# A hybrid of convolution, masked attention and gated blocks on one core: attention scores by 32-row strips, transposed before the exponential, divided at the output

## The reference

```python
x = x + conv(group_norm(x), weight)          # 51x51 depthwise
t = to_tokens(x)                             # (16, 256, 32)
t = t + masked_attention(layer_norm(t))      # spikes of a scan pick the visible columns
t = t + ffn_steps(layer_norm(t))
# masked_attention, per image:
scores = Q @ K.T / sqrt(32), -inf where the mask or the spikes forbid it
w = nan_to_num(softmax(scores)); out = (w @ V) @ Wo + bo
# ffn_steps: 33 steps, each
op = argmax(h[0, 0, :19])                    # the first token of the first image picks the weights
if attn_mask[op]: h = softmax(q @ k.T * scale) @ v @ wo[op]
if ffn_mask[op]:  h = relu(h @ w1[op] + b1[op]) @ w2[op] + b2[op]
```

## Time and profile before

| what | us |
|---|---|
| three runs, median (lowest to highest) | 200.62 (198.45 to 200.82) |
| the profiled execution, span from its first to its last instruction | 199.1 |
| PE busy | 166.5 |
| DVE busy | 134.3 |
| ACT busy | 111.3 |
| POOL busy | 64.1 |

### The profile page before, as it was taken

The page is one execution under the profiler, slowest core; times in us unless marked ns, Lnnn a source line. Parts: engine busy times, 40 slices in busy tenths (PEclk is TensorE's granted clock), DMA queues, the critical chain, the costliest instruction groups (busy, mean ns, idle before and its releaser), DMA issues.

```text
span 199.1 us, 4262 instructions
## 1 busy us (share of the span) xinstructions
PE 166.5 (84%) x1255; PEld 112.6 (57%) x1256; DVE 134.3 (67%) x382; ACT 111.3 (56%) x324; POOL 64.1 (32%) x153
## 2 busy tenths in 40 slices
PE   7999989693898998879929679999867699998770
PEld 5779744241685776647412468776533587775320
DVE  1364578819938889896506388898756689789481
ACT  3464511429767656555405568675655877664670
POOL 8940000100061555453600005655510036556300
PEclk9999999969579999999966999999999999999997
DMA  5900000000000000000000100000000000000003
GB/s 158 315 3 0 3 0 3 0 3 2 0 2 0 2 0 3 0 0 18 3 7 2 20 0 0 0 0 0 0 0 15 0 0 0 0 0 0 0 0 110
DMA packets 3020, 3.33 MB, mean 17 GB/s; under 512 B 889, under 2 KB 2361, under 8 KB 3002
## 3 DMA queue, kind: packets, MB, share of 16 engines
q1 hardware_dynamic: 2858, 2.85, 4.8%
q10 hardware_dynamic: 144, 0.25, 0.4%
HBM read 2.58 MB, written 0.53 MB: 16 GB/s over the span
## 4 chain that ended last, share of the span: by engine, by line
PE 60%; DVE 16%; issue 9%; ACT 8%; POOL 2%; DVEq 1%; ACTq 1%; POOLq 0%
PE bank L555 17%; PE bank L528 8%; PE bank L615 5%; PE bank L542 5%; ACT qz L981 4%; PE bank L679 4%; PE bank L813 3%; PE bank L512 3%; DVE big L1269 3%; PE bank L633 3%; PE bank L600 2%; POOL prob L448 2%; PE bank L694 2%; ACT qz L1050 1%; ACT prob L905 1%
## 5 line engine op out<-in xcount | busy, mean ns | idle before, releaser
L448 POOL TENSOR_SCALAR prob<-prob,einv 128x256 f32<-128x256 f32 x96 | 44.7, 478 | 60.6 <-DVE einv L1264 60.4
L1269 DVE COPY big<-bank 128x512 f32<-128x512 f32 x48 | 32.9, 685 | 5.7 <-PE bank L528 5.7
L905 ACT ACTIVATE prob<-bank,nmax 128x256 f32<-128x256 f32 x64 | 29.8, 473 | 11.6 <-DVE nmax L1256 11.6
L528 PE MATMUL bank<-ident,prob 128*128 128x128 f32 x192 | 30.2, 280 | 6.5 <-POOL prob L448 6.4
L555 PE MATMUL bank<-hT,qz 128*128 128x256 f32 x128 | 32.7, 383 | 0.0
L528 PEld LDWEIGHTS bank<-ident,prob 128*128 128x128 f32 x192 | 21.4, 140 | 18.2 <-POOL prob L448 14.1
L1256 DVE TENSOR_REDUCE nmax<-bank 128x2 f32<-128x512 f32 x32 | 21.6, 687 | 4.8 <-PE bank L555 4.6
L555 PEld LDWEIGHTS bank<-hT,qz 128*128 128x128 f32 x128 | 22.3, 190 | 3.6 <-issue 1.6
L905 ACT ACTIVATE prob<-minus,nmax 128x256 f32<-128x256 f32 x32 | 16.0, 500 | 8.9 <-DVE nmax L1253 7.9
L555 PE MATMUL bank<-kt,qz 128*128 128x256 f32 x64 | 16.5, 386 | 0.9 <-ACT prob L905 0.9
L905 ACT ACTIVATION_READ_ACCUMULATOR prob<-bank,nmax 128x1 f32 x64 | 12.9, 202 | 0.0
(11 more groups left out here) (173 smaller groups left out, 256.8 us busy)
## 6 DMA issues: line engine op xcount, KB each, us to landing
xrev<-xrev_dram SPq DMA_DIRECT2D x1, 512.0 KB, 4.5
xin<-xtok_dram SPq DMA_DIRECT2D x1, 512.0 KB, 5.0
out_dram<-outT SPq DMA_DIRECT2D x2, 256.0 KB, 3.3
maskc<-maskc_dram SPq DMA_DIRECT2D x1, 256.0 KB, 4.8
kx<-kx_dram ACTq DMA_DIRECT2D x1, 248.0 KB, 3.1
wx<-wx_dram SPq DMA_DIRECT2D x1, 216.0 KB, 2.9
constf<-constf_dram SPq DMA_DIRECT2D x1, 186.0 KB, 4.6
wa<-wa_dram SPq DMA_DIRECT2D x3, 56.0 KB, 1.8
```

The source lines that it names most:

```text
L448: last = nc.gpsimd.tensor_scalar(prob[b % NPB][:, ih, :], prob[b % NPB][:, ih, :], einv[:, b, ih:ih + 1], 1.0, ALU.mult, ALU.mult)
L528: mm = pe.transpose(bank[2 + b % 2][:, jh * S + ih * P:jh * S + (ih + 1) * P], prob[b % NPB][:, ih, jh * P:(jh + 1) * P], ident)
L905: e = nc.scalar.activation(prob[b % NPB][:, ih, :], scores, ACT.Exp, bias=nmax[:, b, ih:ih + 1], scale=-1.0 if masked else 1.0, accum_out= ...
L1269: nc.vector.tensor_copy(flat(probT[b % NTB]), bank[2 + b % 2][:, :]).then_inc(s_PT, 1)
```

## The change

1. Queries are stored as projected (`qT`, one instruction per group), and scores contract over 32 rows: `score_pe` uses the strip of its image, two images at a time, into banks 0 to 3.
2. In the masked attention the masked scores go to one of six buffers `sh`; in the loop ACT copies the scores there, and DVE takes the maximum from the copy. POOL subtracts the maximum in place. PE turns the shifted scores into banks 4 and 5, and ACT makes the exponential of 128x512 from PSUM straight into `probT` (16 buffers).
3. Row sums come from PE: the weighing gets as many matmuls again with a column of ones, into the other half of the same bank. In the masked attention a matmul of a tiny constant starts that sum. DVE takes the reciprocal of 128x256 and multiplies while it drains.
4. The sums of the residual move to POOL for groups 0 and 1 (after images 12 and 15) and stay on DVE for 2 and 3.
5. The loop's body has the plain block first, then reads kind again and goes on to the attention in the same pass. The exponential's table is asked for once ahead of the loop.
6. In a block with attention the outputs of groups 0 and 1 stand before the second half of the hidden layer, and the weighing of group 3 before them.
7. The ring of tasks has two banks; `w1` comes with `wf` already in four strips, placed by one copy, on POOL in blocks with attention. The memset of `qz` is gone.

```diff
-        RING = 3
-        SCORES = (0, 1, 4)
-        AHEAD = len(SCORES)
+        RING = 2
+        YBANKS = (6, 7)
...
-        ATTY = "AAAA"
+        ATTY = "DDDD"
-        LPRE = "ADAD" + "ADAD"
+        LPRE = "AAAA" + "ADAD"
...
-                    last = nc.gpsimd.tensor_scalar(prob[b % NPB][:, ih, :], prob[b % NPB][:, ih, :], einv[:, b, ih:ih + 1], 1.0,
-                                                   ALU.mult, ALU.mult)
+                    last = nc.gpsimd.tensor_scalar(sh[b % NSH][:, ih, :], sh[b % NSH][:, ih, :], nmax[:, b, ih:ih + 1], 1.0,
+                                                   ALU.subtract if masked else ALU.add, ALU.mult)
...
+        def score_pe(pe, b, h, keys):
+            g, rows, at_row = strip(b)
+            mm = pe.matmul(bank[b % 4][:, h * S:(h + 1) * S], qT[rows, g, h * P:(h + 1) * P], keys[rows, g, :],
+                           start=True, stop=True, tile_position=at_row)
+            if h == NH - 1:
+                mm.then_inc(s_S, 1)
+        def scores_pe(pe, bs, keys):
+            for h in range(NH):
+                for b in bs:
+                    score_pe(pe, b, h, keys)
...
         def weigh_pe(pe, base, t, k0, g):
+            t.drained(pe, k0 + max(g - 1, 0))
+            wait(pe, s_P, base, GB * (g + 1))
+            out = bank[YBANKS[g % 2]]
...
+            if t is st:
+                pe.matmul(out[:, S:2 * S], onesq[:, :], tiny[:, :], start=True, stop=False)
+            for jh in range(NH):
+                for q in range(GB):
+                    mm = pe.matmul(out[q * C:(q + 1) * C, S:2 * S], onesc[:, :], probT[g * GB + q][:, jh, :],
+                                   start=t is not st and jh == 0, stop=(jh == NH - 1), tile_position=(0, q * C))
...
+        def attention_pe(pe, base, t, k0, keys, ahead, masked):
+            ahead()
+            for n in range(B // 2):
+                if n + 2 < B // 2:
+                    wait(pe, s_nm if masked else s_cp, base, 2 * n + 2 - (0 if masked else B))
+                    scores_pe(pe, (2 * n + 4, 2 * n + 5), keys)
+                turn_pe(pe, base, 2 * n)
+                if n % 2 == 0 and n:
+                    weigh_pe(pe, base, t, k0, n // 2 - 1)
+                turn_pe(pe, base, 2 * n + 1)
...
+            def before_spikes():
+                scores_pe(pe, (0, 1, 2, 3), kt)
+                pe.wait_ge(s_spk, 1)
...
+                    def ahead():
+                        product_pe(pe, t, 0, bda[:, :], hT[:, 0, :], S)
+                        product_pe(pe, t, 1, bda[:, :], hT[:, 1, :], S)
+                        t.drained(pe, 1)
+                        scores_pe(pe, (0, 1, 2, 3), hT)
+                        product_pe(pe, t, 2, bda[:, :], hT[:, 2, :], S)
+                        product_pe(pe, t, 3, bda[:, :], hT[:, 3, :], S)
                         for g in range(NG):
                             values(t, NG + g, hT, g, bdv[:, :])
...
+                with pe.If(kind == 3):
...
+                    token0(r)
+                    hidden(r, 0)
+                    token0_row()
+                    weigh_pe(pe, att, t, len(LPRE), NG - 1)
+                    k = K_HF + GB + 1
+                    t.drained(pe, k - 1)
+                    outputs(t, k, (0, 1))
+                    t.drained(pe, k)
+                    hidden(r, 1)
...
+            def copy_scores(b):
+                wait(act, s_S, base, b + 1)
+                if b >= NSH:
+                    wait(act, s_T, base, b - NSH + 1)
+                nc.scalar.activation(flat(sh[b % NSH]), bank[b % 4][:, :], ACT.Copy).then_inc(s_cp, 1)
...
+                if not masked and b + 4 < B:
+                    copy_scores(b + 4)
+                wait(act, s_T, base, b + 1)
+                nc.scalar.activation(flat(probT[b]), bank[4 + b % 2][:, :], ACT.Exp, scale=-1.0 if masked else 1.0).then_inc(s_P, 1)
...
+            def normed_output(t, k, g, to):
+                t.filled(dve, k)
+                link(nc.vector.reciprocal(sinv[:, g, :], bank[YBANKS[g % 2]][:, S:2 * S]))
+                return nc.vector.tensor_tensor(to[:, g, :], bank[YBANKS[g % 2]][:, 0:S], sinv[:, g, :], ALU.mult)
...
+            def attention_dve(base, masked, output, early=()):
+                for b in range(B):
                     row_max(base, b, masked)
+                    if b == 3:
+                        for e in early:
+                            e()
+                    if b in (10, 14):
+                        output((b - 10) // GB)
```

More of the change, by code:

```diff
@@ L470, in _, with residual, residuals @@
                     nc.gpsimd.tensor_tensor(vg, vg, rep(bvo[:, :], GB), ALU.add).then_inc(s_vb, 1)
-            attention_pool(pool)
+            def residual(g):
+                wait(pool, s_dd, 0, count("D", STATIC[:K_ATT + g + 1]))
+                wait(pool, s_da, 0, count("A", STATIC[:K_ATT]))
+                nc.gpsimd.tensor_tensor(outT[:, g, :], outT[:, g, :], yn[:, g, :], ALU.add).then_inc(s_resP, 1)
+            def residuals(b):
+                if b >= 12 and (b - 12) % 3 == 0:
+                    residual((b - 12) // 3)
+            attention_pool(pool, True, residuals)
             reg_att = pool.alloc_register("pool_att")
@@ L716, in _, with first_token0 @@
             pe.wait_ge(s_tabmove, 32)
-            attention_pe(pe, 0, st, K_ATT, kt, spare)
+            def before_spikes():
+                scores_pe(pe, (0, 1, 2, 3), kt)
+                pe.wait_ge(s_spk, 1)
+                st.fill_wait(pe, K_CNT)
+                pe.matmul(st.bank(K_CNT)[:, 0:S], onesb[:, :], spk[:, :], start=True, stop=True).then_inc(s_task, 1)
+                for h in range(NH):
+                    transposed_pe(pe, K_RES + h, tok, h)
+                spare(bank[5], 6)
+            def first_token0():
+                pe.wait_ge(s_resP, 1)
+                pe.wait_ge(s_cen, 1)
+                pe.wait_ge(s_nm, B)
+                pe.matmul(FIRST0[0:1, C:2 * C], outT[:, 0, 0:1], centre[:, 0:C], start=True, stop=True).then_inc(s_row0, 1)
+            attention_pe(pe, 0, st, K_ATT, kt, before_spikes, True)
+            first_token0()
             def centred(g):
-                wait(pe, s_dd, 0, count("D", STATIC[:K_ATT + g + 1]))
+                if g < 2:
+                    pe.wait_ge(s_resP, g + 1)
+                else:
+                    pe.wait_ge(s_resD, g - 1)
                 pe.matmul(bank[CENTREB[g]][:, 0:S], centre[:, :], outT[:, g, :], start=True, stop=True).then_inc(s_rc, 1)
@@ new lines, in hidden, with outputs @@
+                def hidden(r, gp):
+                    for q in range(GB):
+                        rows = slice(q * C, (q + 1) * C)
+                        if (gp, q) == (1, GB - 1):
+                            pe.wait_ge(s_rowc, r)
+                        pe.matmul(bank[HBANK[gp][q]][:, :], w1r[rows, :], flat(hT[rows, 2 * gp:2 * gp + 2, :]),
+                                  start=True, stop=True, tile_position=(q * C, 0)).then_inc(s_task, 1)
+                def outputs(t, k, ns):
+                    for i, n in enumerate(ns):
+                        for q in range(GB):
+                            mm = pe.matmul(bank[ZBANK[n]][q * C:(q + 1) * C, 0:S], w2s, relu[:, q, n, :],
+                                           start=True, stop=True, tile_position=(0, q * C))
+                        mm.then_inc(s_task, 1)
@@ L1034, in _ @@
             deviation(NG - 1)
+            nc.scalar.activation(table[:, :], eps[0:1, :], ACT.Exp)
             with act.While(lambda: act.snap(reg_code) < NONE):
@@ L1041, in _, with token0 @@
                 r = act.snap(reg_r)
[L1042 to L1055 removed]
+                def token0(r):
                     act.wait_ge(s_w1z, r)
@@ L1073, in ffn, with hidden @@
[L1073 to L1075 removed]
+                def hidden(t, k, gp):
+                    for q in (0, 2):
+                        t.filled(act, k + q)
+                        nc.scalar.activation(relu[:, q, 2 * gp:2 * gp + 2, :],
+                                             bank[HBANK[gp][q]][:, :].rearrange("p (g s) -> p g s", g=2),
+                                             ACT.Relu, bias=b1s).then_inc(s_da, 1)
@@ new lines, in outputs @@
+                def outputs(t, k, ns):
+                    for i, n in enumerate(ns):
+                        t.filled(act, k + i)
+                        nc.scalar.activation(hT[:, n, :], bank[ZBANK[n]][:, 0:S], ACT.Identity, bias=b2s).then_inc(s_da, 1)
+                with act.If(kind == 1):
+                    t = Tasks(FF, act.snap(reg_task))
+                    token0(r)
+                    hidden(t, 0, 0)
+                    hidden(t, GB, 1)
+                    outputs(t, 2 * GB, (0, 1, 2))
@@ new lines, in _, with queries @@
+                kind = act.snap(reg_kind)
+                r = act.snap(reg_r)
+                with act.If(kind >= 2):
+                    att = act.snap(reg_att)
+                    t = Tasks(LATT, act.snap(reg_task))
+                    def queries(g):
```

(7 more changed lines are left out.)

541 lines of the change are left out of this document (219 added, 322 removed).

## The result

The change made the kernel slower. The changed kernel takes 210.47 us (median of 4 runs, 209.71 to 210.74), the kernel before took 200.50 us on the same chip (198.45 to 200.82); the ratio is 1.051, with an interval from 1.045 to 1.058. The profiled execution has a span of 207.6 us where it was 199.1, and a mean granted clock of 0.879 where it was 0.951. The forecast was 186.0 us with a range from 178 to 198, so the result lies outside of it, on the other side of no change. (In all ratios of this document, executions disturbed by a lower clock than their fellows are left out, so that a median over all runs can lie above what the ratio beside it says.)

The account below looks back on a forecast made before the run. Work per image on PE and chains of waits bound the kernel. Masked block -3.3, plain entry -4.9, its following attention -0.5, two rounds -6.0, third round's jump +0.5: -14.2 from 199.1, span 184.9; forecast 186.0 us, range 178 to 198.

Parts of the forecast that it names:

- POOL has two instructions of 0.478 as before, 15 us: Attention loops: POOL keeps two instructions of 0.478 us per image, 15 us, so PE leads and ACT is close.
- The last turn ends at 83.6: Masked loop: PE's last turn of scores ends at 83.6 us, before at 91.67.
- The term of the scores: Attention loops, PE: strips overlap fully, a pair of images costs 0.86 us, 1.1 with its two tile-form switches.
- rival 3: Scores: two strips don't overlap, a pair costs 1.98 us, reciprocals 2.1; 204 us in all; chance 0.06.
- rival 1: Attention loops: ACT's alternation and the two turned banks keep the old 1.55 us an image; 196 us; chance 0.17.
- stalls and a low clock: Masked loop: 2.0 us and 0.7 us added to PE's 20.0 us of work.
- The masked tail: From last masked turn to last normed group: 13.0 us, before 8.2, ending at 96.6 us.
- The gap: Plain block's entry: PE's 3.9 us of "issue" falls to 0.9, a gain of 3.0 us.
- rival 2: Plain block's entry: the gap stays, being register and condition reads, not the jump; +4.9, 191 us; chance 0.17.
- The gain of 1.9 us from the clock: Plain block's entry: without the gap PE runs at 2.4 GHz instead of 1.2, -1.9 us.
- The rounds: Each round with attention: -6.0 us up to its last turn, +2.9 behind it, -3.0 together.
- The reciprocal: Division at the output on DVE, 128x256: 1.5 us, bounds 0.42 and 2.1; on the path for the last group.

Follow-up runs that it names:

- e1: Changed kernel with the masked shift on POOL as times -1 plus the negated maximum, no subtraction; 197.87 us, ratio 0.987 to the kernel before.
- e2: Changed kernel with POOL subtracting the maximum in the two plain attentions too; 234.39 us.
- e13: Changed kernel with the masked shift's operations swapped: times 1.0 first, then less the maximum; 212.85 us.
- e12: e5 with the last masked group first and, in the rounds, the second values' copy one block earlier on DVE; 193.58 us, ratio 0.958.
- e11: e10 with 9 and 5 spare products in the masked tail and, in rounds, the last group's reciprocal ahead of the gate search; 192.62 us, ratio 0.958.
- e5: e1 with spare products on PE in the waits of the masked tail and the rounds' tails; 194.07 us, ratio 0.965.
- e9: e1 with the masked tail reordered: last group's output before the inverted deviations on DVE, its centring before the first scales on PE; 195.14 us, ratio 0.969.
- e3: Kernel before with only the loop's order changed: plain block first, kind read again, then attention, on PE, ACT and DVE; 198.41 us, ratio 0.986.
- e10: e1 with last group's sums before its values, spare products, last masked group first, and an earlier values' copy in rounds; 196.92 us, ratio 0.955.
- The last version: The kernel of e14; 189.21 us, ratio 0.944 to the kernel before.
- e14: e11 without the seven spare products ahead of the first two groups' outputs in each round; 189.21 us, ratio 0.944.
- e6: e1 with the last group's reciprocal done twice in each of the three attentions; 206.62 us, ratio 1.015.

## Why the prediction was wrong

**The step that failed is the one on the other engines: "POOL has two instructions of 0.478 as before, 15 us".** The count and the shape were right, but the operation was not that of the earlier trace rows, which multiplies: the masked form subtracts. It takes 1.12 us, 35.9 us for the attention, and makes POOL the bound of the masked loop, an engine that none of the four rivals named. Replacing it gives 12.2 us of span (run e1; runs e2 and e13 show that it is the operation), over half of the 22.7 us between forecast and result. The bounds should have been drawn for this instruction too, since the trace of before didn't show it.

**The masked loop.** "The last turn ends at 83.6": 95.88 with the subtraction, 83.29 in run e1. The term of the scores holds: a pair takes 1.06 us (128.65 to 129.71) where 1.1 was taken, so the strips overlap and rival 3 falls; PE is busy for 20.0 of 21 us in the second loop of run e1, so rival 1 falls as well. (The Trainium skill, TensorEngine Tiling, Key Properties, has the array drain when the tiling mode changes; the trace has 1.06 us against 0.86 of pure columns, so some 0.1 us a switch, if none of it is in the turns.) That the end fits so well is in part luck. From the third pair to the end of the last turn PE worked 21.8 us in run e1 where 20.0 were taken, since two turns take 1.03 us (129.71 to 130.74) for 0.88, and it waited 0.7 us where 2.7 were allowed for stalls and a low clock. The start also fits by two misses that cancel: the third pair was forecast at 60.9 and starts at 60.79, but the count came at 56.78 instead of 57.9, and behind PE's wait of 6.39 us for it the clock was 1.2 GHz (0.50 for 57 to 59 us), so that the work between them took 4.0 us for 3.0.

**The masked tail.** Forecast 13.0 us; 17.4 after, 17.2 in run e1. The chain itself is 13.3 to 13.7 us once the clock stays up and the order is mended (runs e12, e11). The excess of run e1 is 4.2 us: 2.9 go when TensorE stays at 2.4 GHz through and behind its wait of 2.12 us (run e5), and 2.0 when the last group doesn't queue behind a wait for another (run e9); the two overlap in part. The forecast wrote the instructions of DVE down in their order, but not the waits that stand between them.

**The entry.** The gap went as forecast, and run e3 shows that the order of the blocks made it, with kind still read again: rival 2 falls. The gain of 1.9 us from the clock wasn't had: the long tail left PE at 1.2 GHz there, and in run e5, at 2.4 GHz, the stretch still takes 8.0 us, because PE then waits for DVE. Against 7.5 us forecast from the layer norm's end to the projection it was 8.25.

**The rounds.** Forecast -3.0 each. In run e1 the first turn comes 8.2 us after the first projection (7.5 forecast; run e10 shows a needless wait of 0.83 us there), the last turn ends at 29.0 (27.4, the turns being slower than taken), and the tail to the next projection takes 12.2 us, 4.3 more than before, where +2.9 was forecast: round 2 takes 41.18 us where it took 41.17. So a round gains 4.3 us up to its last turn and loses them behind it. The reciprocal is a mis-sized term: 1.745 us measured, 1.5 taken. Its slope between 2 and 256 elements, (1745 - 160)/254, is 6.2 ns, where the small ones of the earlier trace rows gave 5.5. But more came from what the term set off: PE waits 1.8 us for it and 1.5 for the relus behind it, and then starts round 3 at 1.2 GHz (2.04 and 2.09 us at 161.98 and 163.96, for 1.13 and 1.15 in round 2). There the first turn comes 10.5 us after the projection in run e1, 2.3 later than in round 2. The chain behind the last turn is near its forecast where only its own length counts: 11.1 us to the last sum for 10.5. The forecast held the clock at 2.4 GHz in the rounds, though it had priced that very effect at the entry.

**The table.** No load came back into the loop:

```profile
98.16 1.28 ACT L1075 ACT_TABLE_LOAD   x1
...
110.17 1.28 ACT L1082 ACT_TABLE_LOAD   x1
```

These are the only two of the execution after 50 us, and both lie ahead of the loop. (The Trainium skill, ScalarE: Activation LUTs, Table sets, has relu, copy and identity in every set; the trace of the changed kernel agrees. The kernel before had a load at the first relu of each block all the same, L1059; why isn't shown.)

In sum: 184.9 us of span forecast; +12.2 for the subtraction, and for the rest, by run e1, +3.9 masked loop and tail, +0.6 entry, +3.0 round 2, +3.9 round 3, -1.0 behind it. That is 207.5 us, where the span is 207.6; without the subtraction 195.3, where run e1 has 195.4.

What strips, the later exponential and the division are worth by themselves isn't shown. Run e1, the whole change without its subtraction, is at 0.987 of the kernel before, and run e3, the order of the blocks alone, at 0.986: with the tails as they stood, the rest of the change gave nothing that can be told beyond that order. The last version is at 0.944, but its fillings, early sums and new orders were never tried on the kernel before, so how much of the 5.6% needs strips and division stays open.

## What to carry to other kernels

A group's duration belongs to its operation as well as to its shape: an engine that is idle today can become the bound by a change of one operation that looks free, so bound each instruction whose operation the trace doesn't show. A mean over a group that covers several stages hides this; split it by stage. And price a new wait of 1.5 to 2 us on TensorE twice: once for itself, and once for the slower clock of what follows. Here a few spare products bought that back in most places (run e5), and cost time where they outlasted the wait (runs e11 and e14). Last, when a change has several parts, measure the cheapest part alone: here the order of the blocks alone did as much as the whole change without its subtraction.

## What the runs showed of the hardware

- POOL's `tensor_scalar` on 128x256 fp32 in SBUF took 478 to 484 ns as the mean of one with add and multiply, in either order, and 1144 to 1155 ns with a subtraction in the first or second place (runs e1, e2, e13). Times -1 and an addition did the same work at 479 (run e1).
- DVE's reciprocal of 128x256 out of PSUM took 1745 ns alone and 1757 the second time in a row (run e6).
- TensorE was at 1.2 GHz in stretches behind waits of 1.5 to 2.1 us in the tails, and stayed at 2.4 GHz when these waits held spare products (runs e1 and e5). In the masked tail it fell again in run e10, with 5 of them, and in run e14, with 9, but not in run e11, with the same 9 and the same code there. What exactly makes it fall isn't settled by these runs.
- TensorE's first record of the plain block started 0.07 us after the last normed group when that block's code stood first in the loop's body (run e3), and 3.47 us after it when the attention's code stood ahead (the kernel before).
